# Gate and up projections in three column groups (512, 512, 384), gate ahead of up, with new orders of opening and loop

## What is computed

```python
x = x + xattn(layernorm(x), ctx, ctx, Wt, Wp, Wg, Wz, gamma, beta)
x = x + ffn(layernorm(x), w_gate, w_up, w_down)

# xattn: t = Wt @ ctx, p = Wp @ q, g = Wg @ ctx over the 256 rows; 8 groups of 32 rows;
#        att = sum(p * g) * 0.125 per group; y = Wz @ (att * t) per group,
#        normalised per group, * gamma + beta, + ctx
# ffn:   fp4_linear(v, w) = fp4(v) @ fp4(w).T, 512 -> 1408 (gate, up) and 1408 -> 512 (down)
#        h = silu(gate) * up;  out = fp4_linear(h, w_down)
# fp4:   blocks of 16 along the last axis, scale = max|.| / 6, rounded to 0, .5, 1, 1.5, 2, 3, 4, 6
```

## Time and profile before

| | before |
|---|---|
| median of 3 runs | 1803.06 us (1802.68 to 1804.97) |
| profiled execution, its time | 1802.96 us |
| profiled execution, its span | 1801.2 us |
| TensorE busy | 1738.4 us, 97% |
| VectorE busy | 1611.7 us, 89% |
| ScalarE busy | 705.7 us, 39% |
| POOL busy | 694.8 us, 39% |
| mean granted TensorE clock | 0.993 |

### The profile page before, as it was taken

The page is one execution under the profiler, slowest core; times in us unless marked ns, Lnnn a source line. Parts: engine busy times, 40 slices in busy tenths (PEclk is TensorE's granted clock), DMA queues, the critical chain, the costliest instruction groups (busy, mean ns, idle before and its releaser), DMA issues.

```text
span 1801.2 us, 30830 instructions
## 1 busy us (share of the span) xinstructions
PE 1738.4 (97%) x10124; PEld 1102.1 (61%) x10124; DVE 1611.7 (89%) x2629; ACT 705.7 (39%) x1246; POOL 694.8 (39%) x1069
## 2 busy tenths in 40 slices
PE   3799999999999999999999999999999999999996
PEld 3666666666666666666666666666666666666653
DVE  8998899998999999999999998999999999999884
ACT  3654443343334433333443343334433333343321
POOL 6885433334343324333433334343324333433310
PEclk9999999999999999999999999999999999999998
DMA  6002323233232322323323233232322323323122
GB/s 225 33 13 64 69 65 79 55 69 73 63 79 61 73 67 57 79 63 72 70 64 79 53 71 73 63 79 61 73 66 57 78 63 73 69 65 79 40 56 44
DMA packets 281879, 123.04 MB, mean 68 GB/s; under 512 B 252928, under 2 KB 254208, under 8 KB 281856
## 3 DMA queue, kind: packets, MB, share of 16 engines
q1 hardware_dynamic: 281856, 122.74, 28.7%
HBM read 43.03 MB, written 16.78 MB: 33 GB/s over the span
## 4 chain that ended last, share of the span: by engine, by line
PE 91%; DVE 5%; issue 1%; POOL 1%; DMA 1%; ACT 0%; SPq 0%; DVEq 0%; POOLq 0%; ACTq 0%
PE pairs L483 50%; PE work L494 25%; PE pairs L462 10%; PE ubank L462 5%; DVE work L1265 1%; DVE w_rinv L1062 1%; PE pairs L512 1%; DVE x L1108 0%; PE ubank L475 0%; PE ubank L470 0%; DMA raw<-in_L_ffn_w_gate 0%; DVE q L1080 0%; DMA hT_parts<-raw 0%; DVE h L1054 0%; DVE h L1050 0%
## 5 line engine op out<-in xcount | busy, mean ns | idle before, releaser
L483 PE MATMUL pairs<-w_gate_hi,xT_parts 128*128 128x352 f16 x2048 | 628.3, 313 | 5.3 <-DVE h L1212 4.8
L483 PE MATMUL pairs<-w_up_hi,xT_parts 128*128 128x352 f16 x2048 | 628.0, 313 | 0.0
L494 PE MATMUL work<-w_parts,hT_parts 128*128 128x512 f16 x2112 | 468.5, 380 | 12.9 <-DMA hT_parts<-raw 12.9
L832 ACT ACTIVATE early<-pairs,w_unit 128x352 f32<-128x352 f32 x256 | 141.6, 554 | 615.9 <-PE pairs L483 615.9
L494 PEld LDWEIGHTS work<-w_parts,hT_parts 128*128 128x128 f16 x2112 | 204.8, 99 | 257.6 <-issue 24.2
L483 PE MATMUL pairs<-w_up_lo,xT_parts 128*128 128x352 f16 x1024 | 320.4, 313 | 0.0
L483 PE MATMUL pairs<-w_gate_lo,xT_parts 128*128 128x352 f16 x1024 | 320.3, 313 | 0.0
L483 PEld LDWEIGHTS pairs<-w_gate_hi,xT_parts 128*128 128x128 f16 x2048 | 205.5, 100 | 118.3 <-issue 8.5
L483 PEld LDWEIGHTS pairs<-w_up_hi,xT_parts 128*128 128x128 f16 x2048 | 200.4, 98 | 102.6
L1212 DVE SCALAR_TENSOR_TENSOR h<-pairs,w_unit,early 128x352 f32<-128x352 f32 x256 | 148.0, 578 | 69.9 <-ACT early L832 68.6
L1584 POOL TENSOR_TENSOR q_lo<-q,q_hi 128x512 fp32r<-128x512 f32 x64 | 95.6, 1514 | 214.3 <-ACT q_hi L789 214.3
(11 more groups left out here) (154 smaller groups left out, 2914.3 us busy)
## 6 DMA issues: line engine op xcount, KB each, us to landing
x_in<-in_x SPq DMA_DIRECT2D x32, 512.0 KB, 3.4
c_in<-in_ctx SPq DMA_DIRECT2D x32, 512.0 KB, 3.5
out<-early SPq DMA_DIRECT2D x64, 256.0 KB, 2.0
raw<-in_L_ffn_w_down SPq DMA_DIRECT2D x2, 1408.0 KB, 8.9
raw<-in_L_ffn_w_gate SPq DMA_DIRECT2D x2, 1280.0 KB, 8.3
w_parts<-in_L_ffn_w_up SPq DMA_DIRECT2D x2, 1280.0 KB, 9.0
xT_parts<-raw SPq DMA_TRANSPOSE x64, 3.1
hT_parts<-raw SPq DMA_TRANSPOSE x64, 5.2
```

The source lines that it names most:

```text
L483: mm = pe.matmul(pairs[:, pair, n, 0:GW], xT[s][part][:, k, :], w1[n][wpart][:, k, c * GW:(c + 1) * GW], start=(k == 0 and part == 0 and w ...
L494: mm = pe.matmul(obank[:, :], hT[part][:, k, :], w2[wpart][:, k, :], start=(k == 0 and part == 0 and wpart == 0), stop=(k == KH - 1 and pa ...
L832: nc.scalar.activation(silu[:, c % 2, :], pairs[:, pair_of(j, s, c), 0, 0:GW], ACT.Silu, scale=w_unit[:, 0:1]).then_inc(silu_done, 1)
```

## The change

The columns of gate and up are taken in three groups of 512, 512 and 384. Within a group all 12 matmuls of gate come first and then the 12 of up, and each half has a semaphore of its own: silu waits for gate alone, the product for silu and for up. In the loop the first and the third group of every tile use pair 1, the second group and the scores pair 0. The silu buffer alternates over tiles too, and the output buffer moves from `early` into `raw`.

```diff
-    GROUPS = 4
-    GW = H // GROUPS
+    GROUPS = 3
+    GW = 512
+    SPANS = [(c * GW, min((c + 1) * GW, H)) for c in range(GROUPS)]
...
         def pair_of(j, s, c):
-            return int(j * c == 3) if isinstance(j, int) and j < HT else (s + 1 + c) % 2
+            return int(j * c == 2) if isinstance(j, int) and j < HT else (1 + c) % 2
...
             def hidden(j, s, c):
 
                 pair = pair_of(j, s, c)
-                for k in range(KD):
-                    for part, wpart in PARTS:
-                        for n in range(2):
-                            mm = pe.matmul(pairs[:, pair, n, 0:GW], xT[s][part][:, k, :],
-                                           w1[n][wpart][:, k, c * GW:(c + 1) * GW],
+                a, b = SPANS[c]
+                for n, done in enumerate((gate_done, up_done)):
+                    for k in range(KD):
+                        for part, wpart in PARTS:
+                            mm = pe.matmul(pairs[:, pair, n, 0:b - a], xT[s][part][:, k, :], w1[n][wpart][:, k, a:b],
                                            start=(k == 0 and part == 0 and wpart == 0), stop=(k == KD - 1 and part == 1))
-                mm.then_inc(gu_done, 1)
+                    mm.then_inc(done, 1)
...
             def silu_group(j, s, c):
-                act.wait_ge(gu_done, GROUPS * j + c + 1)
+                act.wait_ge(gate_done, GROUPS * j + c + 1)
...
             def gated(j, s, c):
 
                 dve.wait_ge(silu_done, GROUPS * j + c + 1)
+                dve.wait_ge(up_done, GROUPS * j + c + 1)
```

The body on TensorE, with the last batch changed alike:

```diff
                 if more:
-                    pe.wait_ge(h_done, GROUPS * (j - 1) + 3)
+                    pe.wait_ge(h_done, GROUPS * (j - 1) + 2)
                     scores(j + 2, 0)
...
                 hidden(j, 0, 0)
                 if more:
+                    group_means(j + 2)
+                if more:
                     pe.wait_ge(pg_summed, j + 3)
...
                 hidden(j, 0, 1)
-                if more:
-                    group_means(j + 2)
                 pe.wait_ge(h_done, GROUPS * (j) + 1)
                 hidden(j, 0, 2)
-                pe.wait_ge(h_done, GROUPS * (j) + 2)
-                hidden(j, 0, 3)
                 if more:
                     group_spread(j + 2)
-                    pe.wait_ge(h_done, GROUPS * (j) + 3)
+                    pe.wait_ge(h_done, GROUPS * (j) + 2)
                     scores(j + 3, 1)
                 output(j - 1)
```

More of the change, by code:

```diff
@@ L1329, in _ @@
             x_y(0)
-            variance(1)
+            sum_pg(1, 1)
+            weight_max(2, 2)
+            copy_group(1)
+            weight_max(2, 3)
+            ln1_means(1)
+            weight_scales(2, 1)
             x_add(0)
@@ L1333, in _ @@
             x_quant(0)
-            normalise1(1, 0)
-            normalise1(1, 1)
-            x_lo(0)
-            residual(1, 1)
-            weight_max(2, 3)
-            x1_moments(1)
-            weight_round(7)
-            gated(0, 0, 0)
-            x1_mean(1)
-            weight_scales(2, 1)
-            weight_rowmax(2)
-            weight_round(8)
-            normalise2(1)
-            gated(0, 0, 1)
-            x_first(1)
-            weight_top(2)
+            variance(1)
+            x_lo(0)
+            weight_round(6)
+            weight_round(7)
+            residual(1, 1)
+            weight_rowmax(2)
+            normalise1(1, 0)
+            weight_top(2)
+            x1_moments(1)
+            x1_mean(1)
+            weight_unit(2)
+            weight_round(8)
+            gated(0, 0, 0)
+            normalise2(1)
+            x_first(1)
+            normalise1(1, 1)
             x_scales(1)
             x_y(1)
-            weight_unit(2)
             x_add(1)
             x_back(1)
+            gated(0, 0, 1)
             x_quant(1)
+            weight_round(9)
             gated(0, 0, 2)
-            weight_round(9)
+            h_first(0)
+            h_scales(0, 0)
+            sum_pg(2, 0)
             x_lo(1)
-            gated(0, 0, 3)
-            h_first(0)
             weight_round(10)
-            sum_pg(2, 0)
-            h_scales(0, 0)
             h_y(0)
@@ L1374, in _ @@
             sum_pg(3, 1)
+            h_lo(0, 0)
             residual(2, 0)
@@ L1377, in _ @@
             ln1_moments(2, 0)
+            x1_mean(2)
             ln1_moments(2, 1)
+            normalise2(2)
+            copy_group(3)
+            h_lo(0, 1)
+            x_first(2)
             ln1_means(2)
[L1380 to L1390 removed]
+            x_scales(2)
+            x_y(2)
+            gated(1, 1, 1)
+            normalise1(2, 0)
+            x_add(2)
+            variance(3)
+            normalise1(2, 1)
             x_back(2)
+            gated(1, 1, 2)
+            h_first(1)
             x_quant(2)
[L1393 to L1395 removed]
+            x_lo(2)
+            h_scales(1, 1)
             residual(3, 1)
[L1397 to L1400 removed]
             x1_moments(3)
+            x1_mean(3)
             h_y(1)
[L1403 removed]
+            emit(0, 0, 0)
             h_units(1, 1)
[L1405 removed]
             def body(i):
@@ L1441, in body @@
                     ln1_means(i + 2)
-                h_scales(j, 0)
                 if more:
+                    sum_pg(j + 3, 1)
                     residual(j + 2, 0)
-                h_y(j)
+                h_snap_add(j)
+                h_units(j, 0)
                 if ahead:
@@ L1449, in body @@
                     x1_moments(j + 2)
+                h_snap_back(j)
+                emit(j - 1, 1, 16 * (i - 1))
+                h_quant(j, 0)
+                h_quant(j, 1)
+                h_lo(j, 0)
+                if more:
+                    x1_mean(j + 2)
                 if ahead:
                     normalise1(i + 2, 1)
-                h_units(j, 0)
-                h_snap_add(j)
-                if more:
-                    x1_mean(j + 2)
-                h_snap_back(j)
-                if more:
-                    sum_pg(j + 3, 1)
-                h_quant(j, 0)
-                emit(j - 1, 1, 16 * (i - 1))
-                h_quant(j, 1)
-                gated(j + 1, 1, 0)
-                h_lo(j, 0)
                 h_lo(j, 1)
```

426 lines of the change are left out of this document (190 added, 236 removed).

## The result

| | before | after |
|---|---|---|
| median | 1804.01 us (1802.68 to 1805.32, 4 runs) | 1794.39 us (1793.28 to 1796.35, 4 runs) |
| profiled execution, time | 1802.96 us | 1796.35 us |
| its span | 1801.2 us | 1794.6 us |

The ratio is 0.9951 [0.9936, 0.9967]: faster by 0.5%, against a forecast of 1794.8 us. The profiled execution of after was the slowest of its four, so the two spans differ by 6.6 us, the medians by 9.6. Where in the kernel its executions differ, by 3 to 4 us in all, is part of what follows.

What follows compares the result with a forecast made beforehand. The prediction took TensorE, with work for all 51.97 us of a loop pass, to bound the kernel. From the profiled execution, 1802.96 - 3.0 - 5.2 + 0 = 1794.8 us; range 1787 to 1803.

Steps and rivals of the forecast that it cites:

- Matmuls, -3.0: Tiles ahead of the last two: 24 fewer matmuls a tile, same columns, saves 3.0 us over 62 tiles; ends 0 and 3.5.
- the line through 352 and 512 columns: Matmul cost drawn through 149.4 ns (352 columns) and 216.4 ns (512): 0.419 ns a column, so 384 columns take 162.8 ns.
- Loop, no wait: Loop over batches: the new order makes TensorE wait for nothing; smallest slack 1.0 to 1.6 us, at x's transposing DMA.
- D: Rival, loop: x's transposes land late every pass; a 2.2 us delay costs 0.9 x 30 = 27 us, giving 1822; chance 0.10.
- Closing batch, -5.2: End of output(60) to end of output(62): 42.9 us instead of 48.1, so 5.2 us less; ends 0 and 5.2.
- Both stops for the product of VectorE and the slow clock: Closing batch, tiles 62 and 63: TensorE's waits of 2.2 and 0.9 us and the 0.61 granted clock were to go.
- hT(61), xT(63) and hT(62): Closing batch, transposed operands checked: they land about 0.8, 1.7 and 1.1 us before TensorE wants them.
- the time at which TensorE asks (10.4 us): Closing batch: TensorE, with two groups of 5.19 us, wants tile 62's first product at 10.4; it ends at 8.7 us.
- Opening, 0: Up to the start of output(0) at 161.5 us: gains and losses roughly cancel, taken as 0; ends -8 and +8.
- predicted 1.3: Opening: hidden(0), which began at 92.85 us, comes 1.3 us earlier through VectorE's changed list.
- the last output, put at nothing: Behind the closing batch's gain nothing changes: the last output waits as before and takes 9.29 us as now.

## Why the prediction was right, step by step

- *Matmuls, -3.0*: measured -3.6 from output(0) to output(60), which is 60 tiles; for 60 the prediction's step gives -2.9. The mechanism was right and the term too small: the line through 352 and 512 columns has a fixed part of 2.0 ns a matmul, where the pass shows 0.12 us for 48, or 2.5 ns. A difference of two nearly equal rates hangs on the last digit: 0.02 us more in the piece of 96 matmuls would have made the fixed part 2.7 ns. By the Trainium skill (TensorE: Matmul & The Clock Gate, "Back-to-back issue gap") the estimate was 3.7 for the 62 tiles; the trace agrees with its 2.5 ns (0.120 us for 48 matmuls), and has 2.8 where matmuls of 256 columns were put back.
- *Loop, no wait*: right. The transposing DMA of x has 1.6 us of slack, predicted 1.0 to 1.6. The run with x_lo late shows what its loss costs: 0.8 us in each pass for an excess of 0.65. D's price, the excess alone (27 us for 0.9), was the right mechanism and too low by what the matmuls behind each wait lose.
- *Closing batch, -5.2*: -4.0. Both stops for the product of VectorE and the slow clock went, as counted. The step that failed is the list of what else TensorE asks for. I followed hT(61), xT(63) and hT(62), and not xT(62). In the loop 4.2 us of scores stand between output(j) and hidden(j+2); in the closing batch there are none, so the transpose is wanted that much earlier. The kernel before had the same lack of cover and no time to spare, as SP's timeline shows:

```profile
1724.30 1.34 SPq L376 DMA_TRANSPOSE xT_parts<-raw  x1
```

There the DMA was issued 3.8 us after output(60) began at 1720.47, and with 3.1 to 3.3 us to landing it came just as output(60) ended, at 1727.62. In the kernel after it was issued 5.0 us after the start of output(60) (1722.68 and 1717.68), 1.2 us later, since x_quant and h_scales now stand behind the last product and ahead of x_lo. The run with both moved takes the wait away.

- *Why the stops went*: I named emit behind h_units, x1_moments and x1_mean, and had the wider groups only in the time at which TensorE asks (10.4 us). That order alone is worth 2.6 us in the old kernel and nothing in the new one, where the wider groups already leave VectorE the room (one profiled execution of each). In this the prediction was right in the sum and incomplete in the reason.
- *Opening, 0*: +0.8 in the two profiled executions. Equal code there starts output(0) anywhere from 159.3 to 162.5 us, so neither this +0.8 nor its sign is a property of the change. hidden(0), which began at 92.85 before, began at 91.23 in the kernel after, 1.6 us earlier (predicted 1.3), but at 89.73 in its other profiled execution, so that this agreement is luck. Whether the new order of the opening is better stays open: only two executions with the old one were profiled (161.49, 163.48), and it was not tried by itself.
- *The rest*, +0.2, is the last output at its varying clock (9.29 and 9.39 us) and small steps beside it.

The medians differ by 9.6 us where the stretches give 6.6. The missing 3 us are of the size of the opening's scatter; in the run of the kernel after once more the medians were 8.0 us apart (1802.57 and 1794.60). That the forecast of 1794.8 lies 0.4 us from the median of 1794.39 is therefore in part luck. Like with like, the profiled executions, it is -8.2 predicted and -6.6 measured: the matmuls gave 0.6 us more than their term, the closing batch 1.2 less, and the opening and the last output, put at nothing, took 1.0.

## What to carry to other kernels

Where one engine is busy all the way, count its instructions as well as its columns, and check by an edit that puts back only the count. When a loop's order is laid out anew, go through the passage from the loop into its last pass with every operand of the bound engine, since work that gave cover in the loop is missing there. And a step that is moved takes along what waits for it in every queue, the one that issues DMAs included.

## What the runs showed of the hardware

**VectorE and POOL.** Of VectorE's 87 us the products' smaller number explains 12.8 (148.0 to 135.2 us). The rest lies in operations that are the same in both kernels and take another time. Groups by form, before and then after: the quantising product of x, its low part, and normalise2.

```profile
L1058 DVE SCALAR_TENSOR_TENSOR xq<-xn,x_scale 128x512 f32<-128x512 f32 x64 | 76.5, 1196 | 1.2
L1204 DVE TENSOR_TENSOR raw<-xq,raw 128x512 f16<-128x512 f32 x64 | 66.5, 1039 | 0.3 <-ACT raw L773 0.3
...
L1122 DVE TENSOR_SCALAR xn<-x,ln_mv,ln_rs 128x512 f32 x58 | 31.3, 539 | 0.0
```

```profile
L1099 DVE TENSOR_SCALAR xn<-x,ln_mv,ln_rs 128x512 f32 x58 | 58.7, 1011 | 12.8 <-POOL ln_rs L1533 12.8
...
L1181 DVE TENSOR_TENSOR raw<-xq,raw 128x512 f16<-128x512 f32 x64 | 44.5, 696 | 1.4 <-ACT raw L757 1.4
...
L1035 DVE SCALAR_TENSOR_TENSOR xq<-xn,x_scale 128x512 f32<-128x512 f32 x64 | 44.0, 687 | 1.1
```

The first two fell from 1.20 and 1.04 us to 0.69 and 0.70 in the mean, 54 us in all; the multiply on xn and h_unit fell by 20 and 30 us more; normalise2 rose from 0.54 to 1.01 us, 27 us. In the timeline of the kernel after one can see where the last comes from:

```profile
1004.02 0.54 DVE L1099 TENSOR_SCALAR xn<-x,ln_mv,ln_rs 128x512 f32 x1
...
1035.65 1.48 DVE L1099 TENSOR_SCALAR xn<-x,ln_mv,ln_rs 128x512 f32 x1 [0.44 <-POOL ln_rs L1533]
```

At 1004.02 POOL has nothing to do; at 1035.59 its q_lo begins. So the new order moved the meetings of the two engines from some operations to others and left fewer of them. The Trainium skill (GPSIMD Engine Reference, the table's row on SBUF interfaces) says that the two engines share them; the trace agrees in that POOL's own time fell too, from 694.8 to 621.9 us. Half of that is one operation on 128x1 elements, ln_rs (L1614, then L1585), whose mean fell from 862 to 291 ns; in one pass of the kernel before it takes 1.54 us at 1029.62 and 0.19 at 1055.69. A second of that kind rose, by 14 us. Which of the other operations met which is not separated here, and no run changes this order alone. TensorE gained nothing from it in the loop: it was busy all the way in both kernels.

**The clock.** After its last stop of 12.9 us TensorE needs 8.95 to 9.97 us for 33 matmuls in the eleven profiled executions that have this stop without dead work, and 7.30 when dead matmuls fill the stop: 2.1 us for an edit that changes no result. And ahead of scores(0), after 10.67 us without work, the profile's column says a granted clock of 1.00 while the first fourteen matmuls follow each other at 0.43 us and the last ones at 0.23, a factor of 1.9, close to that between the two levels, 1.2 and 2.4 GHz. With dead work in front all 18 follow each other at 0.23 us. There the pace of equal instructions tells what the column does not.
